# Four record buffers instead of two, and a record load every 3.55 count pieces

## The chip, the cores and the metric

The kernel runs on one core of a Trainium2 chip. The core has five engines with queues of their own: TensorE (PE; its weight loads are shown as PEld), VectorE (DVE), ScalarE (ACT), GpSimd (POOL) and SyncE (SP). They meet only through semaphores. Sixteen DMA engines serve the transfers of all of them. The metric is the device time of one launch in microseconds (us); lower is better.

## The reference

The program is a graph network on 12,500 nodes and 400,000 edges, 64 features wide. Edges are sorted by destination.

```
deg_out, deg_in = counts of src, dst;   out_norm, in_norm = rsqrt(max(deg, 1))
for W, b in three layers:                     # graph convolution
    x = elu((segment_sum((x * out_norm)[src], dst) * in_norm) @ W + b)
x1 = layernorm(x_in + x)
ea  = edge_attr @ W_edge.T + b_edge           # edge_attr: 400000 x 16
agg = segment_sum(relu(x1[src] + ea), dst)
h   = relu(batchnorm((x1 + agg) @ W1.T + b1))
out = layernorm(x1 + h @ W2.T + b2)
```

## The kernel before

The work has three stages. **Stage one** (0 to about 1,950 us) builds, from one-hot matmuls, a table of counts: how many edges go from each source node to each destination node. It is stored in device memory by window of 512 destinations (`counts`). **Stage two** (about 1,950 to 4,670 us) is the three graph convolutions as dense matmuls with these counts. It makes 75 passes (25 windows in each of three layers; `DENSE`). A pass m reads its window's counts in seven pieces (`PIECES`) of 14 source blocks, and TensorE makes 14 matmuls with each piece, 98 in a pass (L2182). The last pass is the last window of the nodes, which is only 256 columns wide instead of 512.

**Stage three** (from about 4,675 us) is the edge layer. The nodes' windows 0 to 4 hold many edges each. For them the edges' records (16 attributes, source, destination: 18 words) have to lie in device memory ordered by window and source block (`sorted_recs`). That ordering is made during stage two, beside the matmuls. There are 1,430 tiles of 128 edges. For each tile, TensorE counts in its rank turns (`rank_turn`, 24 in a pass from m = 1 on, L2157 and L2164) which row each edge gets, and VectorE reads that out (L1444, L1450). Then GpSimd scatters the tile's 128 records to their rows with one indirect DMA (`put_records`, L1051). The ranks of all 1,430 tiles are done in pass 60.

The records themselves come to the core in lots of ten tiles (`GRAN`), 143 lots. SyncE issues the load of a lot (`take_records`, L796), and this is where the order matters. SyncE's queue is one list: it issues the loads of the count pieces (`load_piece`, L789), each of which waits until TensorE has finished with the piece that lay in that place one pass before (`s_pused`). Between them it issues the loads of the lots. Counting the pieces of pass 1 as slots 0 to 6, those of pass 2 as 7 to 13, and so on to slot 517 for the last piece of pass 74, lot g is issued in the first slot not below 3.75 g (`TAKE_EVERY`). Lots 0 and 1 are issued ahead of stage two. What is left after slot 517 is issued right behind the loop. Two buffers hold the lots (`taken`), and the load of lot g waits until all ten scatters of lot g-2 have landed (`s_put`).

Behind the lots' loads, SyncE stores the last rows of the node table (`store_rows`, L802), which GpSimd's gathers of stage three wait for. Before stage three, SyncE and VectorE wait for all scatters. GpSimd's own program is a straight list: for each lot, wait for its load, then twice wait for five keys and issue five scatters.

Of the kernel before, what the change touches and what calls it, by code (L numbers as in the profile page):

```python
# [17 lines left out]
P = 128  # L18
NODES, EDGES, D, EDIM = 12500, 400000, 64, 16
LAYERS = 3  # L20
BLOCKS = -(-NODES // P)
# [4 lines left out]
WINDOWS = -(-BLOCKS // WB)  # L26
PADDED = WINDOWS * WB
TILES = EDGES // P
UNIT = 5
GRAN = 2 * UNIT  # L30
# [141 lines left out]
SETS = [(0, 1), (1, 2)] + [(c, min(c + 15, CHUNKS)) for c in range(2, CHUNKS, 15)]  # L172
# [45 lines left out]
RECORD = EDIM + 2  # L218
# [59 lines left out]

TAKE_EVERY = 3.75

# [8 lines left out]
CHUNK_TILES = 8  # L289
# [61 lines left out]
def gnn_kernel(nc, x, src, dst, dst_rows, edge_runs, edge_recs, attr, w_l0, b_l0, w_edge, b_edge, w1, b1, gamma, beta,  # L351
               w2, b2, out):
    ctx = ExitStack()
    with ctx:
# [110 lines left out]
        def onehot_cols(at, n):  # L465
            return onehot_f[:, at:at + n]
# [42 lines left out]
        ranked = onehot_cols(TEMP + hots * BLOCKS, 2 * BLOCKS).bitcast(F16).rearrange("p (s c) -> p s c", s=2)  # L509
        taken = [onehot_cols(at, GRAN * RECORD).rearrange("p (t r) -> p t r", r=RECORD) for at in (TEMP + (hots + 2) * BLOCKS, FREE + P // 2 + 2 * P)]  # L510
        before_of, after_of = (onehot_cols(FREE + P // 2 + n * P, P).bitcast(F16).rearrange("p (s e) -> p s e", s=2) for n in range(2))
# [175 lines left out]
        s_rowi, ROWI0 = s_find, len(SETS)  # L687
        s_put, PUT0 = s_near[2:4], [16 * (b - a) for a, b in SETS[2:4]]
        PUT_END = [PUT0[s] + 16 * GRAN * len(range(s, RANKED // GRAN, 2)) for s in range(2)]
        s_take, TAKE0 = [s_load, s_w], [32, 16 * (6 * LAYERS + 2 + CHUNK_TILES + 6)]  # L690
        s_base, BASE0 = s_iota, 2
# [54 lines left out]
        def _(sp):  # L746
# [45 lines left out]
            def take_records(g):  # L792

                if g >= 2:
                    sp.wait_ge(s_put[g % 2], PUT0[g % 2] + 16 * GRAN * (g // 2))
                sp.dma_start(taken[g % 2], edge_recs[:, g * GRAN:(g + 1) * GRAN, :]).then_inc(s_take[g % 2], 16)  # L796

# [47 lines left out]
            for m, (n, i, w) in enumerate(DENSE):  # L845
                for k in range(PIECES):
                    if m or k >= 3:
                        load_piece(m, k)
                    if m >= 1 and taken_now < RANKED // GRAN and taken_now * TAKE_EVERY <= (m - 1) * PIECES + k:
                        take_records(taken_now)  # L850
                        taken_now += 1
                if n == LAYERS - 1 and i >= 3:
                    store_rows(i - 3)
# [29 lines left out]
            def sorted_edges():  # L883

                for s in range(2):
                    sp.wait_ge(s_put[s], PUT_END[s])
# [55 lines left out]
        def _(pool):  # L942
# [100 lines left out]
            def put_records():  # L1043

                for g in range(RANKED // GRAN):
                    pool.wait_ge(s_take[g % 2], TAKE0[g % 2] + 16 * (g // 2 + 1))
                    for n in range(2):
                        pool.wait_ge(s_rowi, ROWI0 + g * 2 + n + 1)
                        for k in range(UNIT):
                            t = (g * 2 + n) * UNIT + k  # L1050
                            G.indirect_dma_start(out=sorted_recs[:, :], out_offset=bass.IndirectOffsetOnAxis(ap=keys_of(t, t + 1).bitcast(I32), axis=0),  # L1051
                                                 in_=taken[g % 2][:, n * UNIT + k, :], in_offset=None).then_inc(s_put[g % 2], 16)

# [49 lines left out]
        def _(dve):  # L1103
# [189 lines left out]
            def feature_tops():  # L1293

                dve.wait_ge(s_w, TAKE0[1])
                for n in range(LAYERS):
# [328 lines left out]
            def sorted_edge_sums():  # L1625
# [61 lines left out]

                for s in range(2):
                    dve.wait_ge(s_put[s], PUT_END[s])
# [30 lines left out]
            with V.If(flagged > 0):  # L1720
                for c in (es[GIN].msg[0], es[GIN].msg[1], es[GIN].p3[0], es[GIN].p3[1]):
                    dve.sem_inc(c, 1)
                for s in range(2):
                    dve.wait_ge(s_put[s], PUT_END[s])
# [728 lines left out]
```

## Time and profile before

| what | us |
|---|---|
| median of three runs | 7608.19 (7603.3 to 7616.36) |
| span of the profiled execution | 7586.7 |
| launch around it (median less span) | 21.5 |
| PE busy in the span | 5556.9 (73%) |
| POOL busy in the span | 3774.9 (50%) |
| stage two, about | 1950 to 4670 |

The profiled execution's span is 7586.7 us; the page gives no other time of that execution, so the 21.5 us between it and the median is what lies around the span and any difference between executions. Busy times of the engines overlap. PEclk is the granted TensorE clock as a share of 2.4 GHz; 0.5 is 1.2 GHz, and a number between them is a stretch in which both occurred. An idle time is followed by what ended it; "issue" means that the engine waited for nothing that the profile shows.

### The profile page before, as it was taken

How to read it: one execution, taken by the hardware profiler on the slowest of the kernel's cores; microseconds unless marked ns; L12 is line 12 of the kernel's file. 1: busy time of each engine (PE TensorE's matmuls, PEld its weight loads, DVE VectorE, ACT ScalarE, POOL GpSimd, SP SyncE). 2: the span in 40 equal slices, each digit the busy share in tenths (PEclk: the TensorE clock that was granted, in tenths of full speed). 3: DMA queues.
4: the chain of work that ended last, by engine and by line, in shares of the span. 5: the costliest groups of instructions: out<-in, count | busy, mean ns of one | idle time of the engine just before them, and what ended most of it. 6: DMA issues, size and time to landing. Idle time of an engine off the chain costs nothing.

```text
span 7586.7 us, 112214 instructions
## 1 busy us (share of the span) xinstructions
PE 5556.9 (73%) x39907; PEld 3224.8 (43%) x39908; DVE 4274.3 (56%) x14548; ACT 2271.1 (30%) x4057; POOL 3774.9 (50%) x3824
## 2 busy tenths in 40 slices
PE   6599799997777777778777774666766666665666
PEld 5366566665433333333433332333433333333334
DVE  5488888899533333333444112666666665555556
ACT  2487688873100000000001111333333322222223
POOL 4323233354354544545554556565655666665663
PEclk9799899999888988888888886888888888878887
DMA  2333333331555655556556661111111111111111
GB/s 99 140 130 119 120 142 137 118 118 64 177 173 188 197 177 180 186 186 195 184 185 193 218 207 41 32 34 33 33 33 33 34 33 32 33 33 32 32 32 34
DMA packets 438341, 828.25 MB, mean 109 GB/s; under 512 B 161611, under 2 KB 266983, under 8 KB 430951
## 3 DMA queue, kind: packets, MB, share of 16 engines
q1 hardware_dynamic: 305430, 713.88, 27.9%
q0 software_dynamic: 117952, 81.54, 5.1%
q10 hardware_dynamic: 14400, 25.61, 1.2%
q8 instruction: 323, 5.29, 0.3%
q14 instruction: 236, 1.93, 0.1%
HBM read 621.34 MB, written 199.35 MB: 108 GB/s over the span
## 4 chain that ended last, share of the span: by engine, by line
PE 24%; another core or an unknown queue 14%; issue 13%; DVE 11%; PEld 2%; ACT 1%; PEldq 0%; DVEq 0%; ACTq 0%
PE banks L2182 10%; PE banks L2344 4%; DVE tmp L1673 4%; PE banks L2271 2%; PE banks L2304 2%; PEld banks L2182 2%; DVE onehot L1660 2%; DVE rows_f L1652 2%; PE banks L2324 2%; PE banks L2331 1%; PE banks L2164 1%; DVE rows_f L1680 1%; DVE rows_f L1665 1%; PE banks L2157 1%
## 5 line engine op out<-in xcount | busy, mean ns | idle before, releaser
L1086 POOL DMA_INDIRECT rows_f<-table,src_key x1725 | 1708.4, 990 | 1103.4 <-DVE rows_f L1652 604.3
L1051 POOL DMA_INDIRECT sorted_recs<-onehot,rows x1280 | 1235.5, 965 | 1260.6 <-DMA onehot<-edge_recs_dram 718.7
L2182 PE MATMUL banks<-wide,rows_f 128*128 128x512 fp8e4 (+1 forms) x4900 | 1268.1, 400 | 355.4 <-issue 352.3
L1867 ACT ACTIVATE wide<-banks 128x784 fp8e4<-128x784 f32 x1563 | 1205.6, 825 | 484.6 <-PE banks L2104 340.6
L1006 POOL DMA_INDIRECT onehot<-edge_runs_dram,rows_f x472 | 596.2, 1263 | 1149.1 <-DVE onehot L1196 935.9
L2104 PE MATMUL banks<-rows_f 128*128 128x196 f16 (+2 forms) x7525 | 1004.1, 258 | 223.6 <-ACT wide L1867 138.7
L2104 PEld LDWEIGHTS banks<-rows_f 128*128 128x128 f16 x7525 | 708.5, 152 | 612.1 <-ACT wide L1867 401.9
L2271 PE MATMUL banks<-w_edge_blk,rows 80*128 80x320 f32 x690 | 337.4, 578 | 762.9 <-DVE rows_f L1652 521.6
L1444 DVE SCALAR_TENSOR_TENSOR onehot<-banks,onehot 128x98 f16<-128x98 f32 (+2 forms) x1113 | 295.6, 266 | 989.9 <-PE banks L2164 504.1
L1342 DVE TENSOR_TENSOR rows_f<-hid 128x1024 f16<-128x1024 f16 (+1 forms) x1016 | 679.4, 669 | 300.8 <-PE banks L2104 169.5
L1645 DVE TENSOR_SCALAR rows_f<-banks,iota_p 128x512 f16<-128x512 f32 x294 | 220.7, 751 | 1067.0 <-remote 638.8
L2182 PEld LDWEIGHTS banks<-wide,rows_f 128*128 128x128 f16 x4900 | 454.9, 103 | 817.2 <-issue 510.3
L2069 PE MATMUL banks<-wide,onehot 128*128 128x392 fp8e4 x3125 | 791.5, 334 | 9.2 <-issue 8.9
L2182 PE MATMUL banks<-wide,hid 128*128 128x512 fp8e4 (+1 forms) x2450 | 650.1, 401 | 126.3 <-issue 125.2
L1347 DVE TENSOR_TENSOR rows_f<-rows_f,tmp 128x1568 f16<-128x1568 f16 (+1 forms) x874 | 714.4, 817 | 0.0
L2344 PE MATMUL banks<-tmp,rows_f 128*128 128x512 f16 x2058 | 676.6, 485 | 0.0
L1673 DVE TENSOR_SCALAR tmp<-iota_win,rows 128x512 f16<-128x512 f16 x2058 | 638.0, 379 | 0.0
L1899 ACT ACTIVATE rows_f<-banks 128x512 f16<-128x512 f32 (+1 forms) x294 | 160.0, 544 | 1146.8 <-remote 671.6
L2271 PEld LDWEIGHTS banks<-w_edge_blk,rows 80*128 80x128 f32 x690 | 126.0, 228 | 825.3 <-issue 824.7
L2157 PE MATMUL banks<-onehot 128*128 128x98 f16 (+2 forms) x1113 | 244.1, 219 | 160.2 <-DVE onehot L1444 101.1
L2344 PEld LDWEIGHTS banks<-tmp,rows_f 128*128 128x128 f16 x2058 | 233.5, 120 | 295.3 <-issue 198.3
L1660 DVE TENSOR_SCALAR onehot<-iota_win,dst_key 128x224 f16<-128x224 f16 x1725 | 353.6, 287 | 0.0
(345 smaller groups left out, 7312.1 us busy)
## 6 DMA issues: line engine op xcount, KB each, us to landing
wide<-counts SPq DMA_DIRECT2D x504, 896.0 KB
counts<-wide SPq DMA_DIRECT2D x50, 3136.0 KB
rows_f<-table,src_key POOLq DMA_INDIRECT x1725
sorted_recs<-onehot,rows POOLq DMA_INDIRECT x1280
sorted_recs<-rows SPq DMA_DIRECT2D x28, 640.0 KB
rows<-attr_dram SPq DMA_DIRECT2D x345, 40.0 KB
onehot<-edge_recs_dram SPq DMA_DIRECT2D x143, 90.0 KB
agg_a<-attr_dram ACTq DMA_DIRECT2D x50, 250.0 KB
```

The lines of the kernel that those rows point to most:

```text
L1006: G.indirect_dma_start(out=stage[:, c % STAGES, j, :], out_offset=None, in_=edge_runs[:, :], in_offset=bass.IndirectOffsetOnAxis(ap=run_id ...
L1051: G.indirect_dma_start(out=sorted_recs[:, :], out_offset=bass.IndirectOffsetOnAxis(ap=keys_of(t, t + 1).bitcast(I32), axis=0), in_=taken[g ...
L1086: G.indirect_dma_start(out=g_rows[:, n % ROW_RING, k, :], out_offset=None, in_=table32[:, :], in_offset=bass.IndirectOffsetOnAxis(ap=src_k ...
L1342: V.tensor_tensor(lo_ring[:, s, :, 0:size], iota_lots[:, :, 0:size], lo_cols[:, n:lot.end].rearrange("p (o n) -> p o n", o=1).to_broadcast ...
L1347: V.tensor_tensor(key_ring[:, s, 0:size * cells].rearrange("p (n j e) -> p n j e", n=size, e=2), iota_key[:, 0:cells].rearrange("p (o j e) ...
L1673: last = V.tensor_scalar(c_hot[:, s, k, :], iota_win[:, :], c_dst[:, s, k:k + 1], None, ALU.is_equal)
L1867: A.activation(win_counts[o.half % 2][:, :, d0:d0 + o.quads * QUAD].rearrange("p b (q c) -> p b q c", c=QUAD), counted, ACT.Copy, scale=UN ...
L2069: M(out_ps.rearrange("p (b d) -> p b d", d=QUAD), ident16[:, :], win_counts[o.half % 2][:, :, d0:d0 + QUAD], start=False, stop=False)
L2104: last = M(octet_ps[n % 2][:, q, at:at + item.width * BLOCKS], lo, key, start=fresh[q], stop=True, skip_group_check=True)
L2182: last = M(acc_d[m % 2].rearrange("p (h d) -> p h d", h=2)[:, 0:h, :], layer_rows[n][:, block, :], pieces[:, PLACE[k], 0:h, c * HALF:(c + ...
L2271: M(g_ps, g_attr[:, n % ATTR_RING, :], w_edge_blk[0:UNIT * EDIM, 0:UNIT, :].rearrange("p k f -> p (k f)"), start=True, stop=True).then_inc ...
L2344: last = M(c_acc, c_two[:, s, k, :], c_hot[:, s, k, :], start=False, stop=False)
```

## The change

The records get four buffers. The two new ones lie in cells that the in-degree rows use until the end of pass 0, so SyncE waits once, between the first two pieces of pass 1, for `s_flagsum`, and then loads lots 2 and 3. From lot 4 on, lot g is issued in the first slot not below 3.55 g, and waits for the scatters of lot g-4. The places that wait for the scatters' end wait for four semaphores instead of two.

```
-TAKE_EVERY = 3.75
+TAKEN = 4
+TAKE_EVERY = 3.55
...
+        taken_cells = (TEMP + (hots + 2) * BLOCKS, FREE + P // 2 + 2 * P, 0, GRAN * RECORD)
+        taken = [onehot_cols(at, GRAN * RECORD).rearrange("p (t r) -> p t r", r=RECORD) for at in taken_cells]
...
-                if g >= 2:
-                    sp.wait_ge(s_put[g % 2], PUT0[g % 2] + 16 * GRAN * (g // 2))
-                sp.dma_start(taken[g % 2], edge_recs[:, g * GRAN:(g + 1) * GRAN, :]).then_inc(s_take[g % 2], 16)
+                if g >= TAKEN:
+                    sp.wait_ge(s_put[g % TAKEN], PUT0[g % TAKEN] + 16 * GRAN * (g // TAKEN))
+                sp.dma_start(taken[g % TAKEN], edge_recs[:, g * GRAN:(g + 1) * GRAN, :]).then_inc(s_take[g % TAKEN], 16)
...
                     if m or k >= 3:
                         load_piece(m, k)
+                    if m == 1 and k == 0:
+                        sp.wait_ge(s_flagsum, 1)
+                        take_records(2)
+                        take_records(3)
+                        taken_now = TAKEN
                     if m >= 1 and taken_now < RANKED // GRAN and taken_now * TAKE_EVERY <= (m - 1) * PIECES + k:
                         take_records(taken_now)
                         taken_now += 1
```

No instruction is added to or taken from TensorE, VectorE (but for its waits), ScalarE or GpSimd; the order on SyncE's queue is what moves. At the end of stage two that queue reads, before (piece loads are `wide<-counts`, lots `onehot<-edge_recs_dram`, the stores of the node table `table<-tmp`):

```order
820 L796 DMA onehot<-edge_recs_dram 128x180 [waits s_near3]
821 L789 DMA wide<-counts 128x896 [waits s_pused4]
822 L789 DMA wide<-counts 128x896 [waits s_pused5]
823 L789 DMA wide<-counts 128x896 [waits s_pused6]
824 L802 DMA table<-tmp 128x4x64 [waits s_dparts]
825 L796 DMA onehot<-edge_recs_dram 128x180 [waits s_near2]
826 L796 DMA onehot<-edge_recs_dram 128x180 [waits s_near3]
827 L796 DMA onehot<-edge_recs_dram 128x180 [waits s_near2]
828 L796 DMA onehot<-edge_recs_dram 128x180 [waits s_near3]
829 L796 DMA onehot<-edge_recs_dram 128x180 [waits s_near2]
830 L802 DMA table<-tmp 128x4x64 [waits s_dparts] x2
831 L802 DMA table<-tmp 128x2x64 [waits s_dparts]
```

and now:

```order
813 L792 DMA wide<-counts 128x2x896 [waits s_pused0]
814 L792 DMA wide<-counts 128x2x896 [waits s_pused1]
815 L799 DMA onehot<-edge_recs_dram 128x180 [waits s_near4]
816 L792 DMA wide<-counts 128x2x896 [waits s_pused2]
817 L792 DMA wide<-counts 128x2x896 [waits s_pused3]
818 L792 DMA wide<-counts 128x2x896 [waits s_pused4]
819 L792 DMA wide<-counts 128x2x896 [waits s_pused5]
820 L792 DMA wide<-counts 128x2x896 [waits s_pused6]
```

Five lots stood behind the last piece of pass 74, and none does now: the last lot (815) is issued with pass 73's second piece, and pass 74's pieces and the stores follow without a lot among them. The semaphores `s_near2` to `s_near5` are the scatters' (`s_put`).

In the middle of stage two, on the same queue, before:

```order
486 L796 DMA onehot<-edge_recs_dram 128x180 [waits s_near3]
487 L789 DMA wide<-counts 128x2x896 [waits s_pused2]
488 L789 DMA wide<-counts 128x2x896 [waits s_pused3]
489 L789 DMA wide<-counts 128x2x896 [waits s_pused4]
490 L796 DMA onehot<-edge_recs_dram 128x180 [waits s_near2]
491 L789 DMA wide<-counts 128x2x896 [waits s_pused5]
492 L789 DMA wide<-counts 128x2x896 [waits s_pused6]
493 L789 DMA wide<-counts 128x2x896 [waits s_pused0]
494 L789 DMA wide<-counts 128x2x896 [waits s_pused1]
495 L796 DMA onehot<-edge_recs_dram 128x180 [waits s_near3]
```

and now:

```order
485 L799 DMA onehot<-edge_recs_dram 128x180 [waits s_near4]
486 L792 DMA wide<-counts 128x2x896 [waits s_pused5]
487 L792 DMA wide<-counts 128x2x896 [waits s_pused6]
488 L792 DMA wide<-counts 128x2x896 [waits s_pused0]
489 L792 DMA wide<-counts 128x2x896 [waits s_pused1]
490 L799 DMA onehot<-edge_recs_dram 128x180 [waits s_near5]
491 L792 DMA wide<-counts 128x2x896 [waits s_pused2]
492 L792 DMA wide<-counts 128x2x896 [waits s_pused3]
493 L792 DMA wide<-counts 128x2x896 [waits s_pused4]
494 L799 DMA onehot<-edge_recs_dram 128x180 [waits s_near2]
```

Lots stand three or four pieces apart in both. Before, three of four distances are four pieces and one is three (35 threes, 105 fours from lot 2 on); now 62 are three and 76 are four.

## Rows read from the trace of the kernel before

**Rows 1.** The page: span, engines' busy time, costliest groups (idle before, and its releaser)

```profile
span 7586.7 us, 112214 instructions
...
PE 5556.9 (73%) x39907; PEld 3224.8 (43%) x39908; DVE 4274.3 (56%) x14548; ACT 2271.1 (30%) x4057; POOL 3774.9 (50%) x3824
...
L1051 POOL DMA_INDIRECT sorted_recs<-onehot,rows x1280 | 1235.5, 965 | 1260.6 <-DMA onehot<-edge_recs_dram 718.7
L2182 PE MATMUL banks<-wide,rows_f 128*128 128x512 fp8e4 (+1 forms) x4900 | 1268.1, 400 | 355.4 <-issue 352.3
```

**Rows 2.** Windows: start:end, length, PE, PEld, DVE, ACT, POOL busy, PEclk, DMA, GB/s

```profile
4521.20:4554.50 33.30, 25.88 (x108) 10.90 (x107) 6.17 (x17) 3.77 (x5) 16.95 (x19) 0.85 0.61 206
4554.50:4587.00 32.50, 23.96 (x107) 10.95 (x106) 6.18 (x17) 3.77 (x5) 18.80 (x20) 0.79 0.34 98
4587.00:4666.80 79.80, 18.75 (x81) 8.17 (x79) 6.04 (x17) 2.34 (x5) 52.13 (x55) 0.54 0.09 17
1990.00:4587.00 2597.00, 1962.39 (x10615) 930.73 (x10614) 930.88 (x5494) 136.29 (x215) 1328.22 (x1376) 0.87 0.59 188
```

**Rows 3.** Timeline of SP, end of stage two (start, us, what, count)

```profile
4575.56 0.43 SPq L796 DMA_DIRECT2D onehot<-edge_recs_dram  x1
4576.03 8.04 SPq L789 DMA_DIRECT2D wide<-counts  x3
4584.12 0.43 SPq L802 DMA_DIRECT2D table<-tmp  x1
4584.60 47.17 SPq L796 DMA_DIRECT2D onehot<-edge_recs_dram  x5
4631.82 41.22 SPq L802 DMA_DIRECT2D table<-tmp  x3
4674.67 0.35 SPq L900 DMA_DIRECT2D rows_f<-sorted_recs  x1
```

**Rows 4.** Timeline of PE in the last pass

```profile
4587.88 2.24 PE L2182 MATMUL banks<-wide,rows_f 128*128 128x256 fp8e4 x19
...
4606.55 0.37 PE L2182 MATMUL banks<-wide,rows_f 128*128 128x256 fp8e4 x1 [2.43 <-issue]
...
4663.95 2.31 PE L2182 MATMUL banks<-wide,rows_f 128*128 128x256 fp8e4 x10 [0.30 <-issue]
```

**Rows 5.** Timeline of POOL, the end of stage two and the start of three

```profile
4654.63 0.96 POOL L1051 DMA_INDIRECT sorted_recs<-onehot,hid  x1 [0.30 <-issue]
...
4675.86 0.98 POOL L1086 DMA_INDIRECT rows_f<-table,src_key  x1
...
4720.18 0.95 POOL L1086 DMA_INDIRECT rows_f<-table,src_key  x1 [0.30 <-issue]
```

**Rows 6.** The same stretch, PE

```profile
4694.43 0.57 PE L2331 MATMUL banks<-hid,rows_f 128*128 128x64 f16 x14
4696.33 0.19 PE L2331 MATMUL banks<-hid,rows_f 128*128 128x64 f16 x1 [1.32 <-issue]
...
4726.75 1.11 PE L2285 MATMUL banks<-onehot,rows_f 128*128 128x224 f16 x5
```

**Rows 7.** What POOL waited for in stage two (total us, times, longest)

```profile
POOL sorted_recs L1051 <- DMA onehot<-edge_recs_dram: 775.2, 90, 18.6
POOL sorted_recs L1051 <- DVE rows L1450: 171.5, 16, 79.9
POOL sorted_recs L1051 <- DVE hid L1450: 7.2, 1, 7.2
```

**Rows 8.** Windows: ten scatters that follow at once; twelve such stretches summed

```profile
2440.90:2453.60 12.70, 4.05 (x10) 0.86 (x10) 0.95 (x6) 0.00 (x0) 9.61 (x10) 0.59 0.07 14
...
sum 152.40, PE 36.43 PEld 10.09 DVE 10.37 ACT 2.46 POOL 115.21; mean PE 3.04 PEld 0.84 DVE 0.86 ACT 0.20 POOL 9.60
```

**Rows 9.** Windows: the next ten scatters after each of those, twelve summed

```profile
2467.90:2480.60 12.70, 12.10 (x76) 6.16 (x75) 3.40 (x24) 0.59 (x1) 9.60 (x10) 1.00 0.61 187
...
sum 152.40, PE 120.26 PEld 59.61 DVE 54.69 ACT 5.67 POOL 116.03; mean PE 10.02 PEld 4.97 DVE 4.56 ACT 0.47 POOL 9.67
```

**Rows 10.** Timeline of SP, middle of stage two

```profile
3275.86 0.47 SPq L796 DMA_DIRECT2D onehot<-edge_recs_dram  x1
3276.38 9.17 SPq L789 DMA_DIRECT2D wide<-counts  x3
3285.59 0.47 SPq L796 DMA_DIRECT2D onehot<-edge_recs_dram  x1
```

**Rows 11.** Windows: a pass without a pause of TensorE

```profile
4498.80:4521.20 22.40, 22.14 (x107) 10.45 (x107) 5.97 (x17) 3.77 (x5) 8.41 (x9) 1.00 0.97 322
```

**Rows 12.** Timeline of PE at the end of pass 0

```profile
1984.01 1.13 PE L2136 MATMUL banks<-ident,onehot 98*128 98x98 f32 x8
...
1985.50 0.19 PE L2140 MATMUL banks<-ones_col,scale 128*1 128x1 f32 x2
```

More of the change, by code:

```diff
@@ L509, in gnn_kernel @@
         ranked = onehot_cols(TEMP + hots * BLOCKS, 2 * BLOCKS).bitcast(F16).rearrange("p (s c) -> p s c", s=2)
-        taken = [onehot_cols(at, GRAN * RECORD).rearrange("p (t r) -> p t r", r=RECORD) for at in (TEMP + (hots + 2) * BLOCKS, FREE + P // 2 + 2 * P)]
+        taken_cells = (TEMP + (hots + 2) * BLOCKS, FREE + P // 2 + 2 * P, 0, GRAN * RECORD)
+        taken = [onehot_cols(at, GRAN * RECORD).rearrange("p (t r) -> p t r", r=RECORD) for at in taken_cells]
         before_of, after_of = (onehot_cols(FREE + P // 2 + n * P, P).bitcast(F16).rearrange("p (s e) -> p s e", s=2) for n in range(2))
@@ L687, in gnn_kernel @@
         s_rowi, ROWI0 = s_find, len(SETS)
-        s_put, PUT0 = s_near[2:4], [16 * (b - a) for a, b in SETS[2:4]]
-        PUT_END = [PUT0[s] + 16 * GRAN * len(range(s, RANKED // GRAN, 2)) for s in range(2)]
-        s_take, TAKE0 = [s_load, s_w], [32, 16 * (6 * LAYERS + 2 + CHUNK_TILES + 6)]
+        s_put, PUT0 = s_near[2:6], [16 * (b - a) for a, b in SETS[2:6]]
+        PUT_END = [PUT0[s] + 16 * GRAN * len(range(s, RANKED // GRAN, TAKEN)) for s in range(TAKEN)]
+        s_take, W_LOADED = [s_load, s_w, *s_store], 16 * (6 * LAYERS + 2 + CHUNK_TILES + 6)
+        TAKE0 = [32, W_LOADED, 16 * WINDOWS, 16 * WINDOWS]
         s_base, BASE0 = s_iota, 2
@@ L883, in sorted_edges @@
             def sorted_edges():
-                for s in range(2):
+                for s in range(TAKEN):
                     sp.wait_ge(s_put[s], PUT_END[s])
@@ L1045, in put_records @@
                 for g in range(RANKED // GRAN):
-                    pool.wait_ge(s_take[g % 2], TAKE0[g % 2] + 16 * (g // 2 + 1))
+                    pool.wait_ge(s_take[g % TAKEN], TAKE0[g % TAKEN] + 16 * (g // TAKEN + 1))
                     for n in range(2):
@@ L1051, in put_records @@
                             G.indirect_dma_start(out=sorted_recs[:, :], out_offset=bass.IndirectOffsetOnAxis(ap=keys_of(t, t + 1).bitcast(I32), axis=0),
-                                                 in_=taken[g % 2][:, n * UNIT + k, :], in_offset=None).then_inc(s_put[g % 2], 16)
+                                                 in_=taken[g % TAKEN][:, n * UNIT + k, :], in_offset=None).then_inc(s_put[g % TAKEN], 16)
             rank_tables()
@@ L1293, in feature_tops @@
             def feature_tops():
-                dve.wait_ge(s_w, TAKE0[1])
+                dve.wait_ge(s_w, W_LOADED)
                 for n in range(LAYERS):
@@ L1686, in hidden_stats @@
                     return moments(WINDOW_ENDS[q][2])
-                for s in range(2):
+                for s in range(TAKEN):
                     dve.wait_ge(s_put[s], PUT_END[s])
@@ L1722, in _ @@
                     dve.sem_inc(c, 1)
-                for s in range(2):
+                for s in range(TAKEN):
                     dve.wait_ge(s_put[s], PUT_END[s])
```

## The prediction

> **What bounds the kernel now.** I read the page first [rows 1]: TensorE is the busiest engine and the scatters (L1051) the largest work of POOL. Then the windows of stage two [rows 2]: over 2597 us PE is busy 1962 us, 76%, at a mean clock of 0.87, so a pass is mostly TensorE's own time and the pauses in it. A pass without a pause takes 22.4 us once the ranks are done [rows 11]. The DMA engines are busy 0.59 of that time, so the piece loads are not the limit, and what SyncE does matters only if TensorE or POOL has to wait for it.
>
> The last pass stands out. From 4587.0 to 4666.8 us, 79.8 us go by with 18.75 us of PE work, while POOL issues 55 indirect DMAs [rows 2]. The timeline of SP says why the scatters are there: five lots are issued behind the last piece [rows 3]. That of PE says what it costs: nineteen 256-column matmuls in 2.24 us, then single ones with pauses such as 2.43 us before each, ended by "issue", until the last ten run in 2.31 us again, a few us after the last scatter at 4654.63 [rows 4, 5]. No semaphore is waited for inside a piece. So TensorE is held up while POOL issues indirect DMAs without a break. The start of stage three shows the same with other instructions: POOL issues 30 gathers in a row from 4675.86 to 4720.18, PE falls to single matmuls at 4696.33 and is back at 4726.75 [rows 5, 6]. What in the chip does this, the trace does not tell; I use it as an observed rule: a gapless row of more than about ten to sixteen indirect DMAs all but stops TensorE.
>
> The same happens inside stage two. A lot is ten scatters, 12.7 us. POOL waited 107 times for a load or a key (90, 16 and 1 [rows 7]); so 36 of 143 lots followed their predecessor at once, five of them in the last pass, 31 before. In twelve of these, taken from the timeline of POOL, PE was busy 3.04 of 12.7 us on average, at half clock or little above; in the twelve lots that came next, 10.02 of 12.7, nearly all at full clock [rows 8, 9]. Such a pair arises when the next load comes within 12.7 us, as at 3275.86 and 3285.59, 9.7 us and three pieces apart [rows 10].
>
> **The change part by part.** (1) *No lots behind the last piece.* Lot 142 now falls in slot 505, thirteen pieces ahead of the end. SyncE reaches that place when TensorE has finished the second piece of pass 72, about 4521 us, and its ten scatters end long before the last pass. Of its window in [rows 2], 70 matmuls of 256 columns remain: at 2.24 us for nineteen that is 8.3 us, at half clock 16.5 us, and some 2 us to drain and copy. 79.8 less 10.3 to 18.5 is 61 to 69 us; I take 65. All that follows (the last stores at 4631.82 and later, the first load of sorted records at 4674.67 [rows 3]) hangs on the end of this pass and not on the scatters, so it moves as much. The pass before it (32.5 us with 20 scatters [rows 2]) has none now either; against 22.4 us that is up to 10 us; I take 10, and 0 as its lower end. Together 75 us, bounds 61 to 79.
>
> (2) *Closer lots before.* The five lots, and the one or two that used to come in the last twelve slots, now fall among earlier passes. The ten scatters each are the same work; what counts is how many lots follow at once. From the timelines of SP and POOL I counted, lots 3 to 136, 17 of 34 lots that came three pieces after the last one following at once, and 11 of 100 that came four after. With these shares, 62 threes and 76 fours give 31 + 8 = 39, against 28: 11 more, and I take 10, since the few lots at the start are paced by their keys in both. The ends are none more (if the rate stays what it is whatever the distance), and 27 more (every additional three).
>
> The price of one: 10.02 less 3.04 is 7.0 us of PE's work lost. PE is busy 76% of stage two, so of each us lost some 0.76 should reach the end: 5.3 us. Its ends are 0 (the lost time falls where TensorE would have waited for VectorE anyway) and 8.5 (below). 10 times 5.3 is 53 us, bounds 0 to 27 times 5.3, 143 us.
>
> The clock: in the twelve stretches it stands at 0.50 to 0.68, at 1.00 in most of those after, so the pause of TensorE came first and the slower level, 1.2 GHz, went with it [rows 8, 9]. The Trainium skill, page "TensorE: Matmul & The Clock Gate", section "HAM oscillation — how this bites in real kernels", says that idle gaps put the array back to the half clock and that each return is paid in work at that rate. By it the 3.04 us of busy time are worth only half and the price is 7.0 + 1.5 = 8.5 us each, ten of them 85 us; the trace agrees in the level of the clock, but not in that all of it reaches the end.
>
> (3) *The wait for `s_flagsum`.* Behind it stand lots 2 and 3 and the pieces from pass 1's second on. TensorE gives this signal 1.7 us after its last matmul of pass 0 [rows 12], before it starts pass 1, so pieces 1 to 6 of pass 1 are issued up to 20 us later than now but at most one of them late for TensorE: a piece before this one is 14 matmuls. I take 2 us, bounds 0 to 8.
>
> (4) *Four buffers.* Between lot 6 and the last pass SyncE never stood at a lot's load for its buffer by the timeline; before that it did, for lots 2 to 5, and behind the last piece. I cost this at nothing: the keys, not the records, hold POOL at the start. What the depth does bring is that a backlog of more than two lots is now possible.
>
> The sum is −75 + 53 + 2 = −20 us: a span of 7567, and with 21.5 us around it 7588.
>
> **The rivals.** *B, the closer lots cost nothing.* After a pair POOL pauses and PE runs at full clock, so lost work could be made up where TensorE now waits. Against it: the stretches after a pair are no fuller than a pass at speed. It gives −75 + 2, 7535.
>
> *C, the price is the full one.* By the mechanism just told, TensorE restarts at 1.2 GHz and nothing is made up: ten times 8.5 is 85, less 75, plus 2: +12, 7620. For it speaks that the mean clock of the stage is 0.87; against it, that TensorE waits 24% of the time.
>
> *D, slower: the rows of scatters grow.* A free pass takes 22.4 us and brings 7/3.55 = 1.97 lots, 25.0 us of POOL; before it was 1.87, 23.7 us. Both are above 22.4, now clearly. While SyncE had two buffers it could be at most two lots ahead; with four it may be four, and a row of 30 scatters holds TensorE for 20 us or more, as in the last pass. It decides from 15 more lots that follow at once: 25 of them at 5.3 us are 133, less 75, plus 2: +60, 7668.
>
> *E, the change does not do what it says.* If TensorE's pauses in the last pass did not come from the scatters but from the 256-column form or the half clock there, the pass stays long and only the 5 lots' own waits go: +10 or so from point 2, about 7620. The last ten matmuls at 2.31 us speak against it.
>
> **How the numbers follow.** The forecast has 0.38, B 0.20, C 0.20, D 0.18, E 0.04. A measurement of this kernel can tell about 0.2%, 15 us, from no change. Faster by more: B, and four fifths of the forecast's own spread (−45 to 0): 0.50. Within it: the rest of the forecast and most of C and E: 0.26. Slower: D and the upper part of C: 0.24. The range is 7532 (B with the full 79 us) to 7645, which leaves out the worse half of D.
>
> **What would show it.** Right: no load of a lot behind the last piece; the last pass 10 to 20 us long instead of 79.8; POOL silent in it. For point 2: the number of waits of POOL at L1051's successor for records and keys falls from 107 to about 97 to 103, and the mean pass before the last two grows by about 0.7 us. B: as many pauses and passes of the same length. C and D: mean clock of stage two under 0.87, passes of over 36 us more often, rows of 30 scatters. The forecast is wrong if the last pass stays above 40 us, or if the passes before it get longer by more than 1 us on average.

## The result and the profile after

The changed kernel takes 7709.8 us (median of 4 runs, 7706.12 to 7724.14), the kernel before beside it 7607.9 us. The ratio is 1.0136, with a 95% interval of 1.0117 to 1.0155: slower by 102 us where 20 us less were forecast, and outside the range. Lines of the changed kernel are 8 further down: the scatter is L1059, the load of a lot L799, of a piece L792, the dense matmul L2190.

From the page of the profile after (answers to [rows 1]):

```profile
span 7707.6 us, 112216 instructions
...
PE 5599.6 (73%) x39907; PEld 3239.7 (42%) x39908; DVE 4272.4 (55%) x14548; ACT 2269.4 (29%) x4057; POOL 3763.9 (49%) x3824
...
L1059 POOL DMA_INDIRECT sorted_recs<-onehot,rows x1280 | 1230.3, 961 | 1332.2 <-DMA onehot<-edge_recs_dram 803.0
L2190 PE MATMUL banks<-wide,rows_f 128*128 128x512 fp8e4 (+1 forms) x4900 | 1288.9, 406 | 245.0 <-issue 241.3
```

Windows of the profile after: the last pass but one, the last, and all passes but the last (answers to [rows 2]; columns as there):

```profile
4740.50:4759.90 19.40, 19.14 (x108) 10.35 (x107) 5.97 (x17) 3.77 (x5) 0.00 (x0) 1.00 0.54 162
4759.90:4769.00 9.10, 8.63 (x80) 7.58 (x78) 5.97 (x17) 2.28 (x4) 0.00 (x0) 1.00 0.15 36
1981.70:4759.90 2778.20, 2009.61 (x10592) 940.92 (x10591) 932.58 (x5478) 136.22 (x215) 1374.15 (x1430) 0.83 0.57 177
```

SyncE's timeline at the end of stage two after (answers to [rows 3]):

```profile
4707.19 0.48 SPq L799 DMA_DIRECT2D onehot<-edge_recs_dram  x1
4716.16 18.40 SPq L792 DMA_DIRECT2D wide<-counts  x5
4734.60 0.57 SPq L805 DMA_DIRECT2D table<-tmp  x1
4737.64 19.29 SPq L792 DMA_DIRECT2D wide<-counts  x7
4756.97 17.88 SPq L805 DMA_DIRECT2D table<-tmp  x4
4776.55 0.35 SPq L908 DMA_DIRECT2D rows_f<-sorted_recs  x1
```

POOL's waits in stage two after (us in total, times, longest; answers to [rows 7]):

```profile
POOL sorted_recs L1059 <- DMA onehot<-edge_recs_dram: 879.2, 83, 20.0
...
POOL sorted_recs L1059 <- DVE rows L1458: 149.2, 17, 80.5
POOL sorted_recs L1059 <- DVE hid L1458: 14.8, 1, 14.8
```

The end of the stage came out as forecast and better: no lot behind the last piece, POOL silent in the last two passes, which take 9.1 and 19.4 us instead of 79.8 and 32.5. That is 84 us less. But the passes before them, whose mean length was to grow by 0.7 us, grew by 2.8: from 1994.2 to 4554.5 us in the profile before and from 1981.7 to 4740.5 in the one after, 2560.3 and 2758.8 us for 72 passes. With 12.5 us less before the first pass and 18.7 us more behind the last, −84 + 198 + 6 makes the 121 us between the two spans. The medians are only 102 us apart: the profile before shows an execution about 20 us faster than its median, so the 198 us are the high end. (The 21.5 us that the prediction adds for what lies around the span are mostly this: in the profile after, 1.8 us lie between the span and the time of the same execution.) Two more pairs of profiles of this difference in spacing, with the same windows, have 150 us (`four_375` and `two_355`) and 164 us (`before_again` and `after_again`, below).

### The profile page after: what moved, and what is told of

Same layout as the page of the kernel before. It is cut to its first block, busy times and chain, and to the rows that moved or that the text cites. A ratio compares the mean times of both kernels' runs of the same rounds, so it can differ in the third digit from the quotient of the medians.

```text
span 7707.6 us, 112216 instructions
## 1 busy us (share of the span) xinstructions
PE 5599.6 (73%) x39907; PEld 3239.7 (42%) x39908; DVE 4272.4 (55%) x14548; ACT 2269.4 (29%) x4057; POOL 3763.9 (49%) x3824
## 4 chain that ended last, share of the span: by engine, by line
PE 27%; another core or an unknown queue 16%; issue 13%; DVE 11%; PEld 2%; ACT 1%; DVEq 0%; PEldq 0%; ACTq 0%
PE banks L2190 13%; PE banks L2352 4%; DVE tmp L1681 3%; PE banks L2279 2%; PE banks L2312 2%; PEld banks L2190 2%; DVE rows_f L1660 2%; DVE onehot L1668 2%; PE banks L2332 2%; PE banks L2172 1%; PE banks L2339 1%; PE banks L2165 1%; DVE rows_f L1688 1%; DVE rows_f L1673 1%
## 5 line engine op out<-in xcount | busy, mean ns | idle before, releaser
L1059 POOL DMA_INDIRECT sorted_recs<-onehot,rows x1280 | 1230.3, 961 | 1332.2 <-DMA onehot<-edge_recs_dram 803.0
L2190 PE MATMUL banks<-wide,rows_f 128*128 128x512 fp8e4 (+1 forms) x4900 | 1288.9, 406 | 245.0 <-issue 241.3
L1452 DVE SCALAR_TENSOR_TENSOR onehot<-banks,onehot 128x98 f16<-128x98 f32 (+2 forms) x1113 | 295.7, 266 | 1076.5 <-PE banks L2172 515.6
L2190 PE MATMUL banks<-wide,hid 128*128 128x512 fp8e4 (+1 forms) x2450 | 664.6, 408 | 134.6 <-issue 134.3
L2190 PEld LDWEIGHTS banks<-wide,rows_f 128*128 128x128 f16 x4900 | 459.1, 104 | 714.0 <-issue 415.4
L2190 PEld LDWEIGHTS banks<-wide,hid 128*128 128x128 f16 x2450 | 225.9, 105 | 315.4 <-issue 198.1
```

The source lines that it names most:

```text
L2190: last = M(acc_d[m % 2].rearrange("p (h d) -> p h d", h=2)[:, 0:h, :], layer_rows[n][:, block, :], pieces[:, PLACE[k], 0:h, c * HALF:(c + ...
```

## The experiments

"Passes 0 to 71" below is the time from the node matmuls of pass 0 to those of pass 72. A lot "follows at once" when its first scatter starts within 0.7 us of the end of the one before, counted on POOL's timeline: in passes 0 to 71 this holds for 27 lots in the kernel before and for 51 in the changed one. The kernel before took between 7608 and 7753 us in four groups of runs and about 5930 us in two; each ratio is with the kernel before in the same group.

### Depth and spacing apart

`four_375`: the changed kernel with the old spacing. `two_355`: the kernel before with the new spacing and two buffers.

```diff
 four_375, on the changed kernel      two_355, on the kernel before
-TAKE_EVERY = 3.55                   -TAKE_EVERY = 3.75
+TAKE_EVERY = 3.75                   +TAKE_EVERY = 3.55
```

> The changed kernel with 3.75 pieces between the lots again, four buffers kept. Theory 1 (spacing): what costs is the number of lots that follow their predecessor at once, about 8.7 us each, and it is set by the distances between the loads, not by the buffers. SyncE's slots are then those of the kernel before, so 7608 +/- 12 us, about 33 such lots, five lots behind the last piece and a last pass of about 80 us. Theory 2 (depth): four buffers let POOL's backlog and its rows of scatters grow; then over 7640 us.

Measured: ratio 0.9997 (0.9971 to 1.0023), with 33 lots that follow at once in passes 0 to 71 and a last pass of 80.7 us.

> The kernel before with 3.55 pieces between the lots, two buffers kept. Theory 1 (spacing): as the changed kernel, 7710 +/- 20 us, about 50 lots that follow at once, last pass about 10 us. Theory 2 (depth): two buffers hold the rows short; the end of stage two is won and little lost, at most 7630 us.

Measured: 1.0138 (1.0084 to 1.0193), with 54 such lots and a last pass of 9.2 us. The whole loss comes from the spacing; two more buffers do nothing, and rival D, which needed them, falls.

### Where in the pass the lots stand

Two lots in each pass from pass 3 on, at fixed pieces.

```diff
-if m >= 1 and ... and taken_now * TAKE_EVERY <= (m - 1) * PIECES + k:
+if m >= 3 and ... and k in (2, 6):        # at_2_5: k in (2, 5)
```

> Four buffers, two lots in each pass from pass 3 on, behind the loads of its pieces 2 and 6: so the three-piece distance spans the change of pass, where the kernel before took 17.5 us for three pieces, and the four-piece distance lies in the fast pieces (18 us). Theory 1 (spacing, by phase): about 16 to 25 lots follow at once, the end is as in the changed kernel: 7608 - 84 - 5 to 12 times 8.7, so 7420 to 7480 us. Rival (density): only how many lots stand in a pass counts; 2.0 against 1.97 is as bad as the changed kernel, 7700 us or more.

Measured: 0.9959 (0.9936 to 0.9982), and 0.9959 (0.9935 to 0.9982) in a second group.

> The same with pieces 2 and 5: same number of lots per pass, but now the three-piece distance lies in the fast pieces (12.6 us in the kernel before) and the four-piece distance at the change of pass. Theory 1 (spacing, by phase): 45 to 60 lots follow at once, 7690 to 7780 us, 200 us or more above the kernel with pieces 2 and 6. Rival (density): the same time as that one within 30 us.

Measured: 1.0210 (1.0192 to 1.0229), 182 us above `at_2_6`; density alone would have left them within 30 us of each other. Passes 0 to 71 of `four_375`, `two_355`, `at_2_6` and `at_2_5`, one row of windows from each trace:

```profile
1996.80:4611.50 2614.70, 1950.11 (x10486) 926.27 (x10485) 925.39 (x5461) 132.45 (x210) 1303.81 (x1355) 0.86 0.59 187
```

```profile
1987.30:4751.60 2764.30, 2011.27 (x10485) 933.49 (x10484) 928.73 (x5461) 132.51 (x210) 1378.34 (x1430) 0.83 0.56 176
```

```profile
1991.30:4671.70 2680.40, 1978.55 (x10486) 936.23 (x10485) 934.45 (x5461) 132.51 (x210) 1379.41 (x1430) 0.86 0.58 183
```

```profile
1996.20:4842.40 2846.20, 1983.79 (x10486) 962.37 (x10485) 923.41 (x5461) 132.43 (x210) 1371.18 (x1430) 0.83 0.54 172
```

`at_2_6` and `at_2_5` have the same number of scatters in these passes, and 24 and 69 lots that follow at once: 165.8 us for 45 lots, 3.7 us for each (an estimate, since the lots also stand behind other pieces). Three pieces between a lot and the next do not make a fixed share of pairs: the lots of piece 5, three after those of piece 2, follow at once 68 times of 69; those of piece 2, three after piece 6 of the pass before, 14 times of 70 (in `at_2_6`).

But `at_2_6` was expected far below 7600 us. It has 9 pairs fewer than `four_375` and yet 65.7 us more in these passes: it also has 75 scatters more there (x1430 against x1355 in POOL's column). So a lot seems to cost something even alone. The next run asked for that price.

### The price of a lone lot

```diff
-if m >= 1 and ... and taken_now * TAKE_EVERY <= (m - 1) * PIECES + k:
+if m >= 15 and ... and k in ((2,) if m < 31 else (0, 2, 5)):
```

> The changed kernel with another count of lots per pass: from pass 3 on none, from pass 15 one (piece 2), from pass 31 three (pieces 0, 2 and 5) until all are loaded. Read from the lengths of the passes; two lots per pass are known from the kernel with pieces 2 and 6 (37.7 us in passes 1 to 57). Theory A (only lots that follow at once cost, which the prediction's sum assumed): passes with no lot and with one are 33 to 35 us, hardly apart. Theory B (a lot costs in itself wherever it stands, about 6 us, since the scatters hold other engines' signals up; where the kernel before took 5930 us and nothing was held up, passes were 24.6 us): 24 to 26 us with none, 29 to 32 us with one, 44 to 50 us with three.

Windows of `ramp_0_1_3`: nine passes without a lot, eight with one, 28 with three:

```profile
2123.30:2344.40 221.10, 218.70 (x1389) 112.50 (x1388) 124.14 (x781) 9.04 (x18) 0.00 (x0) 1.00 0.81 263
2377.90:2637.40 259.50, 213.07 (x1236) 105.46 (x1234) 111.11 (x694) 8.04 (x16) 76.83 (x80) 0.88 0.65 204
2951.50:4361.00 1409.50, 853.80 (x4311) 395.16 (x4309) 412.95 (x2495) 52.77 (x83) 810.07 (x840) 0.75 0.45 138
```

A pass is 24.6 us without a lot (the clock at 1.00 throughout), 32.4 with one, 50.3 with three; with two, passes 1 to 57 of `at_2_6` have 37.7. The steps are 7.8, 5.3 and 12.6 us. Theory B holds, with one and three lots just above its bounds: a lot lengthens its pass also when no other is near. The last step contains lots that follow at once, and the second comes from another kernel, so the steps are no exact prices. The whole kernel takes 7885.6 us in the one run, against 7632.8 for the kernel before.

### What the scatters do to the others

Sums of ten windows in `at_2_5`, first 7.6 us from the start of a row of twenty scatters, then 7.6 us from its ninth scatter on:

```profile
sum 76.00, PE 71.93 PEld 37.15 DVE 32.67 ACT 1.37 POOL 57.77; mean PE 7.19 PEld 3.72 DVE 3.27 ACT 0.14 POOL 5.78
...
sum 76.00, PE 7.22 PEld 2.77 DVE 9.45 ACT 0.58 POOL 57.57; mean PE 0.72 PEld 0.28 DVE 0.94 ACT 0.06 POOL 5.76
```

So TensorE is hardly touched by the first six scatters and all but stopped after the eighth. In all rows of the changed kernel between 2032 and 4196 us, single lots too, it starts 5.7 to 6.1 instructions per us during each of the first six scatters, 5.2 during the seventh, 4.3 and 3.2 during the next two and 0.3 to 1.8 from the tenth on (counted on the timelines of PE and POOL). One such row, from the timeline of all engines of `at_2_5` (the row began at 2785.7 us):

```profile
2793.17 0.21 PE L2172 MATMUL banks<-onehot 128*128 128x98 f16 x1
...
2793.22 0.59 PE L2190 MATMUL banks<-wide,rows_f 128*128 128x512 fp8e4 x2
2793.27 0.95 POOL L1059 DMA_INDIRECT sorted_recs<-onehot,rows  x1 [0.31 <-issue]
...
2802.00 0.26 DVE L1452 SCALAR_TENSOR_TENSOR onehot<-banks,onehot 128x98 f16<-128x98 f32 x1 [5.89 <-remote]
...
2805.49 0.36 SPq L792 DMA_DIRECT2D wide<-counts  x1
2805.54 0.58 ACT L1889 COPY agg_a<-banks 128x512 f32<-128x512 f32 x1 [27.48 <-PEq L2206]
...
2805.72 1.87 PE L2190 MATMUL banks<-wide,rows_f 128*128 128x512 fp8e4 x4 [11.91 <-issue]
```

VectorE's instruction at 2802.00 needs only the matmul that ended at 2793.38. TensorE's last matmul before the gap, which ended at 2793.81, frees a piece for SyncE, and SyncE goes on at 2805.49; ScalarE, which waits for the drain behind that matmul, at 2805.54, and TensorE at 2805.72. The two signals whose sender is plain were given 8.6 and 11.7 us before they had an effect. This is what "issue" and "remote" stand for here. That the signals come late, the trace shows; what holds them, it does not.

The 1430 matmuls of L2172 and VectorE's 1430 instructions of L1452 pair off one by one, so the time from the end of one to the start of the other can be read for each. In the changed kernel the median is 0.0 us when the matmul ends during the first to fourth scatter of a row, 1.7 during the fifth, 5.0 during the sixth and 6.9 during the seventh, and the longest is 19.6 us.

Late signals are not all of it. In the last pass of the kernel before, TensorE paused 2.43 us before single matmuls in the middle of a piece, where it waits for no signal [rows 4]. So its own instructions are held up as well, and the common cause of both stays open.

### Half the rows, as many scatters

```diff
-IndirectOffsetOnAxis(ap=keys_of(t, t + 1).bitcast(I32), ...), in_=taken[...][:, n * UNIT + k, :]
+IndirectOffsetOnAxis(ap=keys_of(t, t + 1)[0:P // 2, :].bitcast(I32), ...), in_=taken[...][0:P // 2, n * UNIT + k, :]
```

> The changed kernel with each scatter writing the records of 64 partitions instead of 128: as many scatters and lots, at the same places, half the rows moved. It leaves the other half of the records out. If what a scatter costs goes by its rows (descriptors written and carried out), TensorE no longer stops in rows of scatters and the passes fall from 39 us to 26 to 31 us; if it goes by the instruction, or if GpSimd's instruction takes 0.96 us as before, passes stay within 1.5 us of 39 us.

Passes 0 to 71 of `half_rows`, and its scatters among POOL's groups in stage two:

```profile
1994.20:4797.20 2803.00, 2003.29 (x10486) 941.56 (x10484) 919.41 (x5461) 132.43 (x210) 1284.81 (x1430) 0.83 0.53 172
```

```profile
L1059 POOL DMA_INDIRECT sorted_recs<-onehot,rows x1270 | 1140.1, 898 | 1438.7 <-DMA onehot<-edge_recs_dram 932.3 <-issue 358.5 <-DVE rows L1458 147.9
```

38.9 us per pass in this one run, against 38.3 with all the rows; the kernel leaves the other half of the records out. The price does not go by the rows moved. Whether it goes by the instruction or by its rate, which stays nearly the same here (one each 1.20 us in place of 1.26), the next runs ask.

### A rest ahead of each scatter

```diff
+if t:
+    pool.wait_ge(s_base, BASE0 + 2 + t)
+G.memset(rest, 0.0).then_inc(s_base, 1)      # rest: 152 unused f32 cells of onehot
 G.indirect_dma_start(out=sorted_recs...
```

`after_rest` and `before_rest` have this in the changed kernel and in the one before, `at_2_6_rest` in the one with fixed pieces; `after_rest5` has five memsets ahead of every fifth scatter; `after_rest2` and `before_rest2` have two ahead of each.

> The changed kernel with one short GpSimd instruction (a memset of 128x152 f32 in unused cells, an estimated 0.25 us from the 128x98 and 1x98 memsets of the trace, 0.17 to 0.21 us) ahead of each scatter of the records, so that no row of scatters has one every 1.27 us any more. Nothing else is changed. Theory 1 (what costs is the rate of a gapless row: in the traces TensorE issues about 6 instructions per us up to the seventh scatter of a row and 1 per us from the ninth on, and signals of TensorE and VectorE sent then arrive up to 12 us late, at 2793.38 us sent and at 2802.0 us received in one row): the stops go, passes fall from 38 us to 31 to 34 us (then GpSimd's 20 scatters of 1.6 us set them), and the time to 7350 to 7480 us. Theory 2 (the number of scatters in a row counts, whatever their rate, or GpSimd's own time bounds the loop): the rows become longer, nothing is given back, 7700 to 7850 us.

> The same rests as in after_rest, but five of them in a row ahead of every fifth scatter, so that the total of the rests is the same and five scatters still follow each other every 1.27 us. Theory 1a (a row must not reach the seventh scatter, and a pause of about 1.5 us ends a row): like after_rest, 7350 to 7480 us. Theory 1b (a pause so short doesn't let the held signals out: lots that came after a gap of under 2 us had TensorE at 2 to 4 instructions per us in the traces, against 6 after gaps of over 5 us): in between, 7500 to 7650 us. Theory 2 (number of scatters or GpSimd's time): 7700 to 7850 us.

> The kernel before (two buffers, one lot for every 3.75 pieces) with the rest ahead of each scatter. Theory 1: its 28 lots that follow at once in the loop cost as they do in the changed kernel, and single lots lose TensorE's rate from the seventh scatter on too, so this kernel gains as well: 7350 to 7480 us, the lots behind the last piece (a longer last pass, some 20 us longer by the rests) included. Theory 2: nothing is given back and the last pass grows: 7620 to 7700 us.

> Four buffers, two lots per pass at pieces 2 and 6, with the rest ahead of each scatter. Theory 1: with rests the spacing hardly counts, within 40 us of after_rest, 7340 to 7480 us. Theory 2: as without rests or slower, 7600 to 7700 us.

This group had the kernel before at 5928.8 us, and with that no theory's number could come out. Ratios: `after_rest` 1.0221 (1.0204 to 1.0238), `before_rest` 1.0221, `at_2_6_rest` 1.0231, `after_rest5` 1.0560 (1.0542 to 1.0578). Windows of `after_rest` there, one pass with 18 scatters and most of stage two:

```profile
1969.10:1993.70 24.60, 24.34 (x158) 12.51 (x156) 14.82 (x86) 1.00 (x2) 21.54 (x36) 1.00 0.72 231
1920.00:3744.60 1824.60, 1668.31 (x9866) 843.46 (x9865) 937.74 (x5104) 128.46 (x202) 1604.14 (x2646) 0.97 0.72 250
```

A pass with 18 scatters takes 24.6 us, the length of one with none in `ramp_0_1_3`. TensorE starts 5.7 instructions per us from the tenth scatter of a row on, where it has 0.8 in `before_again`. In that group scatters cost the others nothing that shows, rests are only POOL's time, and what the first four expectations asked stayed undecided. So the kernels were run again.

> The kernel before, unchanged, for its trace on the chip of this group of runs: in the last group it took 5928.8 us, against 7607.9 and 7630.6 us where the other kernels ran. Theory 1 (signals held up during gapless rows of indirect DMAs make the difference, and they are held up on some chips only): at about 5930 us a trace shows TensorE at 5 to 6 instructions per us throughout rows of over ten scatters and count passes of 23 to 26 us; at about 7610 us it stops from the seventh scatter on and has passes of 36 us. Theory 2 (chips differ in another way, in the memory's rate or the clock): the rows look alike on both, and the difference is in transfers or in the granted clock outside the rows.

> The changed kernel, unchanged, beside the kernel before on the chip of this group. Theory 1: where the kernel before takes 7600 us, a ratio of 1.013 as first measured; where it takes 5930 us, lots that follow at once cost nothing, GpSimd's scatters follow each other with few gaps and the end of the loop decides: 0.985 to 1.000. Theory 2: 1.013 on both kinds of chip.

> The changed kernel with a 0.24 us memset ahead of each scatter, beside the kernel before. On a chip where the kernel before takes 5930 us it lost 2.2% (GpSimd without a gap, one scatter each 1.5 us). Where the kernel before takes 7600 us, theory 1 (the rate of a gapless row holds the signals up) expects passes of 31 to 34 us and 7350 to 7480 us; if the rest is too short for that, or if the number of scatters counts, 7700 to 7850 us.

> Four buffers and two lots per pass at pieces 2 and 6, without rests, beside the kernel before: 0.9959 was measured where the kernel before takes 7630 us. Where it takes 5930 us, theory 1 expects no cost of lots at once and so the same as the changed kernel within 0.5%.

This time the kernel before took 7752.7 us, on the chip with the same number as in the group at 5928.8; so it is not one chip against another. `after_again` 1.0105 (1.0074 to 1.0135): the loss repeats, here with 33 and 47 lots that follow at once. Passes 0 to 71 of `before_again` and `after_again`:

```profile
2011.30:4675.50 2664.20, 1979.71 (x10485) 929.18 (x10484) 926.85 (x5461) 132.51 (x210) 1306.40 (x1357) 0.84 0.58 182
```

```profile
2003.10:4831.50 2828.40, 2014.74 (x10486) 939.74 (x10485) 930.20 (x5461) 132.51 (x210) 1377.48 (x1430) 0.82 0.55 173
```

`after_rest_again` 0.9874 (0.9820 to 0.9928), a gain, though far less than forecast: one rest leaves a scatter each 1.37 us, and 493 of the 1430 signals from TensorE to VectorE still take more than 3 us, against 429 in the changed kernel. It is the kernel of `after_rest`, which took 6060.6 us in the other group and takes 7659.4 here.

> The changed kernel with two 0.24 us memsets ahead of each scatter (one gave 0.9874 of the kernel before, and passes of 37.3 us with GpSimd busy all the time). Theory 1 (it is the rate of scatters that holds signals up, each taking about 1.9 us of something shared): a scatter each 1.8 to 1.9 us leaves TensorE free, passes of 36 to 38 us set by GpSimd alone, 7600 to 7700 us with the last lots behind the last piece. Theory 2 (each scatter stops the others for a fixed time, wherever it stands): TensorE at 4 instructions per us as with one rest, no gain, and the lots that are now late come on top, 7700 to 7850 us.

> Pieces 2 and 6 with one 0.24 us rest ahead of each scatter. Without rests this spacing gave 0.9959 of the kernel before, and the changed kernel with rests 0.9874 where the kernel before takes 7600 to 7750 us; if the two gains are of the same kind (rows of over six scatters each 1.27 us) they don't add: 0.980 to 0.990. If they are of different kinds: 0.970 to 0.980. Where the kernel before takes 5930 us: 1.023, as measured.

`after_rest2` 0.9599 (0.9565 to 0.9633), 7318.45 us, and `at_2_6_rest_again` 0.9806 (0.9767 to 0.9845), with the kernel before at 7632.8 us. The first did better than either theory allowed. The second lies at the edge between its two, so it does not tell whether the gains are of one kind. Passes 0 to 71 of `after_rest2`:

```profile
1995.80:4330.60 2334.80, 1866.65 (x10486) 921.44 (x10485) 1000.99 (x5461) 132.68 (x210) 2010.13 (x4177) 0.91 0.60 208
```

What TensorE waited for in `after_rest2` (whole line: us, times, longest), then in the changed kernel:

```profile
PE banks L2195 <- DMA wide<-counts: 453.8, 113, 12.4
PE banks L2195 <- issue: 14.0, 54, 0.3
```

```profile
PE banks L2190 <- issue: 375.3, 200, 19.1
PE banks L2165 <- DVE onehot L1452: 274.7, 104, 9.6
PE banks L2165 <- issue: 112.8, 51, 8.0
```

With two rests a scatter comes every 1.7 us (2334.8 us for 1392 of them). A pass takes 32.4 us instead of 38.3, and TensorE's unexplained waits are all but gone: 14.0 us ended by "issue" in place of 488. None of the 1430 signals from TensorE to VectorE takes more than 2.5 us. What is left is the wait for the load of a piece, and SyncE's waits in passes 0 to 71 say what holds that load, in the changed kernel, in `after_rest_again` and in `after_rest2`:

```profile
SPq L792 <- remote: 1448.7, 158, 22.3
```

```profile
SPq L793 <- remote: 1367.5, 185, 17.5
```

```profile
SPq L800 <- DMA sorted_recs<-onehot,rows: 410.9, 28, 16.2
SPq L800 <- DMA sorted_recs<-onehot,hid: 56.9, 4, 14.9
SPq L793 <- PE banks L2195: 50.3, 18, 4.3
```

The late signals ("remote") are gone there too. Instead SyncE stands at the load of a lot (L800) until its buffer is free. By the timelines 138 of the 139 lots that wait for a buffer are issued within 6 us, mostly 1.2 us, after the end of its tenth scatter, and the pieces behind them follow at once:

```profile
2717.45 0.33 SPq L800 DMA_DIRECT2D onehot<-edge_recs_dram  x1
2717.83 1.38 SPq L793 DMA_DIRECT2D wide<-counts  x3
2733.98 0.33 SPq L800 DMA_DIRECT2D onehot<-edge_recs_dram  x1
2734.36 2.33 SPq L793 DMA_DIRECT2D wide<-counts  x4
```

So GpSimd sets the pace now, by way of SyncE's queue: 1.97 lots in a pass, each ten times 1.65 us, are 32.5 us. POOL never waits for a lot any more. The last scatters run through the last two passes, which are 21.1 and 9.2 us long, and end at 4392 us, 31 us after the last matmul of the stage. Three of POOL's instructions in place of one make the kernel faster by 5.0 to 5.3% than the changed one, by way of the kernel before (0.9599 over 1.0105 or 1.0136).

Two last runs asked whether spacing still matters with rests, and whether the gathers of the edge stage do the same.

```diff
+for r in ...: G.memset(pause[:, :], 0.0).then_inc(s_base, 1)      # two, 44 cells, ahead of each gather
 G.indirect_dma_start(out=g_rows[:, n % ROW_RING, k, :], ...
```

> The kernel before (two buffers, 3.75 pieces) with two 0.24 us memsets ahead of each scatter. The changed kernel with the same two rests gave 0.9599, with passes of 32.4 us and GpSimd without a gap. If the rests take away what made closer lots dear, spacing and buffers no longer matter but for what is left behind the last piece: 0.958 to 0.972. If four buffers or the closer spacing are needed to keep GpSimd fed at this pace: 0.975 to 0.990.

> The changed kernel with two rests ahead of each scatter, and two memsets of 128x44 f32 (an estimated 0.12 us each, from the 1x98 row of 0.17 us) ahead of each of the 1725 gathers of the edge stage, which follow each other in rows of five each 1.27 us. If signals are held up there by the same thing (the edge stage took 2920 to 2940 us here, and about 2280 us in the one group of runs in which nothing was held up), that stage gets shorter by 100 to 400 us: 0.90 to 0.95. If the rate of gathers matters only in rows longer than six, each rest is just GpSimd's time: 0.960 to 0.985.

The kernel before was at 5936.6 us: 1.0926 (1.0908 to 1.0945) and 1.1602 (1.1583 to 1.1622). No theory's number could come out of this group either, so both questions stay open. Under these conditions the rests are a clear loss.

## Why the prediction was wrong

- **Step 1, no lots behind the last piece: right.** Forecast −75 (bounds 61 to 79), measured −84, a little past the upper bound: the last pass took 9.1 us, not 14.8, with the clock at 1.00 in it, and the pass before 19.4. The 22.4 us taken as its free length had nine scatters in it [rows 11].
- **Step 2, closer lots: the step that failed**, +53 forecast and +198 measured (+150 and +164 in the other two pairs of profiles). Three sizes are in it. *The lots moved into the passes* were costed at nothing ("the ten scatters each are the same work; what counts is how many lots follow at once"). `ramp_0_1_3` shows 7.8, 5.3 and 12.6 us for the first, second and third lot of a pass; 7.3 lots moved in (1429 scatters in passes 0 to 71 instead of 1356), at 5.3 to 12.6 us 39 to 92 us, an estimate. *The number that follow at once* rose by 24, not 10 or 11: the share among the threes was taken as fixed at one half (17 of 34) and went to 45 of 62 (fours: 5 of 76), because it depends on which pieces of a pass lie between, as `at_2_6` and `at_2_5` show. *The price of one* was 5.3 us and is 3.7: this error was on the safe side. 24 at 3.7 are 89 us. Together 128 to 181 of the 198; the rest is no larger than the difference between executions (the same 72 passes take 2560.3 us in the profile before and 2614.7 in `four_375`, whose time is the same).
- **How far this split holds.** It is rough: the 12.6 us contain pairs already; `at_2_6` against `four_375` gives 13 us for a moved lot (65.7 us and nine pairs fewer, for 7.5 lots); and `after_again` has only 14 pairs more than `before_again`, yet 164 us. That both terms count, the runs show; how much each, they bound loosely.
- The premise under it, **a row of more than ten to sixteen indirect DMAs stops TensorE**, was right in kind and set too high: signals come late from the fifth scatter on, and TensorE falls off with the eighth. So every lot of ten had its cost already, and the twelve windows "after a pair" [rows 9] hid it, because I compared pairs with other lots and never with a pass without one. The profile had no such pass; the bound for a moved lot should then have run from nothing to the mean excess of a pass over its free length [rows 2, 11], about 7 us a lot (2597 us for 73 passes against 22.4 each, 1.88 lots per pass), and did not.
- **Step 3, the wait for `s_flagsum`: right**, within its bounds of 0 to 8 us: the two passes around it take 78.0 us together against 77.4.
- **Step 4, four buffers cost nothing: right** (`four_375`, 0.9997).
- **Its signs.** The prediction named 1 us more per pass as what would prove it wrong, and it was 2.8; the mean clock fell from 0.87 to 0.83, as C and D had it. One sign came out and misled: POOL's waits for loads and keys fell from 107 to 101, inside the 97 to 103, while the lots that follow at once rose by 24 in passes 0 to 71. But three of the 107 waits and nine of the 101 lie inside a lot, so they do not count pairs; the 36 pairs read from them for the kernel before are 33 on the timeline.
- **The rivals.** B and E fall. C has the right direction but its mechanism, the half clock, is only a part: in `at_2_5` TensorE's busy time falls to 0.72 of 7.6 us, a stop and not a slow run. D has the right sign and place of blame; its mechanism, rows that grow through depth, is refuted by `two_355`.

The sign of the change, put in one line: it takes lots from a place where they cost 11 us each (74 scatters and 84 us in the last two passes), puts them where they cost 5 to 13, and brings 24 pairs on top.

## What to carry to other kernels

Work that "is the same wherever it stands" needs a price for the place it is moved to; make a stretch without it and one with double, and read the difference, before the sum is made. Where a trace shows waits ended by "issue" or "remote" on several engines at once, look at what one engine does without a pause at that time. When a remedy leaves waits with a name, follow the name one queue further: here the load of a piece stood behind that of a lot, and that waited for GpSimd. And a remedy found so should be tried more than once: two rests per scatter gave 4% in the changed kernel here and lost 9% in the kernel before where that ran at 5937 us.

## What the runs showed of the hardware

- While GpSimd issues indirect DMAs one each 1.26 us without a gap, signals between the other engines come late from the fifth on (median 1.7 us, then 5.0 and 6.9, at most 19.6 in the changed kernel), and TensorE falls from about 6 instructions per us to about 1 from the tenth on. One each 1.37 us does the same to the signals (`after_rest_again`, 493 of 1430 over 3 us), one each 1.65 us does not (`after_rest2`, none over 2.5 us). It does not go by the rows moved (`half_rows`). What is held up, the traces do not show; each of these executions was recorded by the profiler, and no run shows whether the recording has a part in it.
- This holds only under some conditions. In two groups of runs the kernel before took 5929 and 5937 us, 22 to 24% less than in the others; the first had the chip number that gave 7753 us another time. In the trace of `after_rest` from there the edge stage took 2285 us (from 3773.1 us to the end at 6057.6) against 2939 in the profile after, with the same instructions. What differs between the groups, no run shows; nor was the changed kernel without rests run there, so its worth under those conditions is open.
